# Edge stage of a graph layer: one loaded number a step for ScalarE's copies, and TensorE's per-step numbers worked out in registers

## The reference, cut to what matters

```python
e = el[src] + er[dst]
e = jnp.where(e >= 0, e, NEG_SLOPE * e)
e_max = jax.ops.segment_max(e, dst, num_segments=N)
exp_e = jnp.exp(e - e_max[dst])
denom = jax.ops.segment_sum(exp_e, dst, num_segments=N)
a = exp_e / jnp.maximum(denom[dst], 1e-16)
msg = feat_v[src] * a[:, :, None]
rst = jax.ops.segment_sum(msg, dst, num_segments=N)
```

## Time and profile before

| | before |
|---|---|
| median of 3 runs | 3522.52 us (3513.96 to 3525.18) |
| the profiled execution | 3480.26 us, span 3478.4 us |
| PE (matmuls) busy | 2417.5 us (69%) |
| DVE busy | 1829.6 us (53%) |
| POOL busy | 1338.1 us (38%) |
| ACT busy | 909.8 us (26%) |
| granted TensorE clock, mean | 0.809 |

### The profile page before, as it was taken

One profiled execution on the slowest core, in us unless ns is written; L12 is line 12 of the kernel. 1 busy time (PEld: TensorE's weight loads), 2 busy tenths in 40 slices (PEclk: granted clock), 3 DMA queues, 4 the chain that ended last, 5 costly groups with the idle time before them and its releaser, 6 DMA issues. The chain is left out here.

```text
span 3478.4 us, 50828 instructions
## 1 busy us (share of the span) xinstructions
PE 2417.5 (69%) x11245; PEld 1803.3 (52%) x11246; DVE 1829.6 (53%) x3903; ACT 909.8 (26%) x1917; POOL 1338.1 (38%) x1406
## 2 busy tenths in 40 slices
PE   3899998666777877777877777777233329999500
PEld 3677776223555555555555555555233328888400
DVE  5544443786666655566556655565353334444433
ACT  0111111011333333333333333333443313333100
POOL 0000000302565555565556555652144342222244
PEclk8899998898888878888788878889555559999755
DMA  3122222644555555655656556653655634444576
GB/s 115 49 68 68 68 68 77 228 167 134 165 162 159 157 164 163 169 160 154 169 164 171 166 154 173 170 163 89 221 134 136 131 76 134 145 145 145 168 257 232
DMA packets 238264, 507.89 MB, mean 146 GB/s; under 512 B 50320, under 2 KB 76432, under 8 KB 238208
## 3 DMA queue, kind: packets, MB, share of 16 engines
q0 software_dynamic: 85936, 274.85, 28.6%
q1 hardware_dynamic: 134752, 196.94, 18.5%
q10 hardware_dynamic: 17520, 35.44, 3.0%
HBM read 394.73 MB, written 112.37 MB: 146 GB/s over the span
## 5 line engine op out<-in xcount | busy, mean ns | idle before, releaser
L618 POOL DMA_INDIRECT arena<-v_table,idx x832 | 917.2, 1102 | 847.1 <-PE ps L1566 670.1
L1566 PE MATMUL ps<-arena 128*128 128x260 f32 x3328 | 975.4, 441 | 315.9 <-issue 289.6
L1566 PEld LDWEIGHTS ps<-arena 128*128 128x128 f32 x3328 | 678.5, 216 | 533.2 <-issue 427.7
L757 ACT ACTIVATE arena<-ps x832 | 501.9, 603 | 1096.2 <-PE ps L1566 668.4
L1182 DVE TENSOR_TENSOR arena<-arena 128x512 f32<-128x512 f32 x832 | 547.1, 683 | 0.0
L1384 PE MATMUL ps<-arena 128*128 (+4 forms) x1994 | 423.8, 336 | 94.3 <-DMA arena<-q_table 73.8
L1389 PE MATMUL ps<-ident,arena 128*128 128x128 f32 x1128 | 213.8, 308 | 328.1 <-DVE arena L1257 257.2
L1384 PEld LDWEIGHTS ps<-arena 128*128 128x128 f32 (+1 forms) x1994 | 275.7, 195 | 224.8 <-issue 115.3
L1389 PEld LDWEIGHTS ps<-ident,arena 128*128 128x128 f32 x1128 | 151.0, 159 | 349.3 <-DVE arena L1257 262.2
L658 POOL DMA_INDIRECT arena<-xn_table,e_idx x105 | 99.3, 945 | 281.5 <-PE ps L1389 265.0
L595 POOL TENSOR_SCALAR ag<-ag 128x1 f32<-128x1 f32 x49 | 10.7, 219 | 502.3 <-DVE ag L999 502.2
(11 more groups left out here) (282 smaller groups left out, 3470.0 us busy)
## 6 DMA issues: line engine op xcount, KB each, us to landing
y_table<-arena SPq DMA_DIRECT2D x105, 256.0 KB, 2.5
arena<-local_table ACTq DMA_DIRECT2D x52, 512.0 KB, 4.2
arena<-in_x SPq DMA_DIRECT2D x98, 256.0 KB, 2.7
arena<-v_table,idx POOLq DMA_INDIRECT x832
v_table<-arena SPq DMA_DIRECT2D x49, 260.0 KB, 2.9
agg<-arena SPq DMA_DIRECT2D x49, 260.0 KB
arena<-agg SPq DMA_DIRECT2D x49, 260.0 KB, 4.6
x_mix<-arena SPq DMA_DIRECT2D x49, 256.0 KB, 2.7
```

The costliest lines, as they stand in the source:

```text
L618: pool.indirect_dma_start(vg[:, j % 2 * U + i, :], None, v_table, bass.IndirectOffsetOnAxis(ap=idx[:, j, i:i + 1], axis=0))\
L757: act.activation(halves(fin[:, bass.ds(dst_, DH)], HALF), halves(ps[:, bass.ds(src_, 2 * D)], D)[:, :, 0:HALF], ACT.Copy).then_inc(s("act_ ...
L1566: last = pe.matmul(ps[:, bass.ds(acc + h * D, HALF)], hot[:, i // V % 2, i % V, :], vg[:, b * U + i, h * HALF:(h + 1) * HALF], start=False ...
```

## The change

Tables: the tables pe_tab, act_tab, d_tab and chunk_tab go. In their place stand first_tab (the tile of each chunk's first step), turn_tab (16 bits for each chunk, one for each step that ends a tile), and room_tab (for ScalarE, one number a step, from which it takes both where to read and where to write). `fin` now has its slots at the same distances as the accumulators and two of them in place of four.

ScalarE: one load of 16 numbers for a chunk; a copy waits for its own copy before and for the matmuls of the step after, and no longer for tile_sum and for the stores. TensorE: for each two chunks it loads four tiles and four bit rows; it works out each step's accumulator, turn and next tile in registers, and in `expanded` the tile of each of the 16 matmuls; at the end of a tile it waits in addition for the stores. The preparation of the next chunk is put after later steps: on TensorE from after 1, 3, 5, 8, 10 to after 5, 7, 9, 12, 11 (`turned_max` now behind `factors`), on VectorE from after 2, 4, 6, 9, 12 to after 5, 7, 9, 11, 13. VectorE builds the first one-hot matrix of a chunk ahead of its wait for the weights (`found`).

```diff
-            def snapshots(t, n):
-                places = looked_up(ENGINE.Activation, act_tab, t * 2, 2 * n, DUMMY * D)
-                counts = looked_up(ENGINE.Activation, act_tab, t * 2 + 2 * ST, 2 * n, 32768)
...
+            def snapshot(t, room):
+                if later(t, 1):
+                    act.wait_ge(*past("act_step", t))
+                act.wait_ge(s("step_mm"), t + 2)
+                act.activation(halves(fin[:, bass.ds(room, DH)], HALF), halves(ps[:, bass.ds(room, 2 * D)], D)[:, :, 0:HALF],
+                               ACT.Copy).then_inc(s("act_step"), 1)
...
+                rooms = looked_up(ENGINE.Activation, room_tab, c * U, U, DUMMY * D)
+                for i in range(U):
+                    snapshot(c * U + i, rooms[i])
+                    if not more:
+                        continue
+                    if i == 8:
+                        factor(c + 1)
+                    elif i == 11:
+                        weights(c + 1, 1 - b)
...
-                    if i == 2:
+                    if i == 5:
                         scored(c + 1, n, q)
-                    elif i == 4:
+                    elif i == 7:
                         run_max(c + 1, n)
-                    elif i == 6:
+                    elif i == 9:
                         linked(c + 1)
-                    elif i == 9:
+                    elif i == 11:
                         joined_max(c + 1, n)
-                    elif i == 12:
+                    elif i == 13:
                         shifted(c + 1, n)
...
-                for i, d in enumerate(tiles):
+                for i in range(U):
                     last = product(prep[:, i * 3 * H:(i + 1) * 3 * H],
-                                   [(hot_t[:, i * P:(i + 1) * P], er_flat[:, bass.ds(d * 3 * H, 3 * H)])])
+                                   [(hot_t[:, i * P:(i + 1) * P], er_flat[:, bass.ds(d * (3 * H), 3 * H)])])
+                    if i < U - 1:
+                        d = next_tile(pe, d, turn_of(pe, bits, i))
...
-            def step(t, i, b):
-                if i % V == 0:
-                    marks[:] = looked_up(ENGINE.PE, pe_tab, t * 2, 2 * V + 1, 2 * D)
-                acc, turn, other = marks[i % V * 2:i % V * 2 + 3]
+            def step(t, i, b, d, turn):
+                acc = held(pe, (d & 1) * (2 * D), 2 * D)
+                other = held(pe, (acc + 2 * D) & (4 * D - 1), 2 * D)
                 pe.wait_ge(s("step_pv"), t + 1)
...
                 with pe.If(turn):
-                    empty(acc, False, True).then_inc(s("tile_sum"), 1)
-                    freed, = looked_up(ENGINE.PE, pe_tab, t + (2 * ST + 2), 1, ST)
+                    empty(acc, False, True)
+                    pe.wait_ge(s("fin_st"), d * 16 + past("fin_st", -16)[1])
+                    freed, = looked_up(ENGINE.PE, tile_tab, d, 1, past("act_step", ST)[1])
                     pe.wait_ge(s("act_step"), freed)
...
-                    if i == U - 1 and ahead:
-                        tiles = tiles_of(c + 2)
-                    step(c * U + i, i, b)
+                    turn = held(pe, (bits >> i) & 1, 1)
+                    after = held(pe, d + turn, NT - 1)
+                    step(c * U + i, i, b, d, turn)
+                    d = after
```

More of the change, by code:

```diff
@@ L60 @@
[L60 to L64, removed]
@@ L745, in weights, with chunk @@
                 act.activation(score_cols(b), score_cols(b), ACT.Exp).then_inc(s("p_exp"), 1)
-            def snapshots(t, n):
-                places = looked_up(ENGINE.Activation, act_tab, t * 2, 2 * n, DUMMY * D)
-                counts = looked_up(ENGINE.Activation, act_tab, t * 2 + 2 * ST, 2 * n, 32768)
[L750 to L760, removed]
+            def snapshot(t, room):
[4 more added lines that the diff above has]
+                               ACT.Copy).then_inc(s("act_step"), 1)
+            def chunk(c, b, r, own):
                 more = not (isinstance(c, int) and c == NCH - 1)
@@ L779, in _ @@
             weights(0, 0)
-            chunks(act, chunk)
+            chunks(act, chunk, lambda c, n: (None,) * n, 0)
             act.wait_ge(s("step_mm"), ST)
@@ new lines, in _ @@
+            step_of(last)
+            in_chunks = [row_.rearrange("o (c i) -> o c i", i=U) for row_ in (turn, aux)]
+            step_of(dve.tensor_tensor(in_chunks[1], in_chunks[0], power_row.unsqueeze(1).broadcast_to([1, NCH, U]), ALU.mult))
+            step_of(dve.tensor_reduce(bits, in_chunks[1], AX.X, ALU.add))
+            dve.tensor_copy(turn_tab[0:1, 0:NCH], bits)
+            dve.memset(turn_tab[0:1, NCH:NCH + 2], 0)
+            dve.tensor_copy(first_tab[0:1, 0:NCH], d_r[:, 0:ST:U])
@@ L1226, in _ @@
             turned_hot(1, 1, 0)
[L1227 removed]
+            chunks(dve, chunk, lambda c, n: chunk_places(ENGINE.DVE, c, n), 0)
             def weights_lo(c):
@@ L1609, in _ @@
             turned_max(0)
-            expanded(1, tiles_of(1))
-            empty(0, True, False).then_inc(s("tile_sum"), 1)
-            chunks(pe, chunk, lambda c, n: looked_up(ENGINE.PE, chunk_tab, c, n, 2 * D))
-            empty((NT - 1) % 2 * 2 * D, False, True).then_inc(s("tile_sum"), 1)
+            expanded(1, *begun[1])
+            empty(0, True, False)
+            chunks(pe, chunk, lambda c, n: chunk_places(ENGINE.PE, c, n), 2)
+            pe.wait_ge(*past("fin_st", 16 * (NT - 2)))
+            empty((NT - 1) % 2 * 2 * D, False, True).then_inc(s("step_mm"), 1)
             def logits(t):
```

167 lines of the change are left out of this document (78 added, 89 removed).

## The result

The changed kernel takes 3714.65 us (median of 4 runs, 3701.60 to 3720.55) against 3518.80 for the kernel before (4 runs, 3513.96 to 3525.18): a ratio of 1.055, with a 95% interval of 1.052 to 1.059. It is slower by 5.5%, outside the forecast of 3450 to 3690; the direction was right. Two repeats gave 1.053 (1.050 to 1.056) and 1.055 (1.052 to 1.058).

A forecast was written before the change was run, and what follows sets the result against it. The prediction took TensorE's sequencer to bound the kernel. Its terms summed to +1.6 us a chunk (+82 us), with -9 for the prologue: 3553 us profiled, scaled to a forecast of 3595 us, range 3450 to 3690.

The forecast's parts named there:

- What bounds the kernel: Edge stage: TensorE sets the pace, and within TensorE its sequencer; a chunk takes 30.9 us.
- The price of 0.10 us: TensorE's sequencer: one register instruction costs 0.10 us, within 0.04 to 0.12.
- Steps 0 to 4: TensorE, chunk's start: a load goes and the slow clock hides some register work, -1.6 us a chunk.
- Steps 4 to 8: TensorE: register work about equals the load it replaces, plus two small matmuls, +0.2 us a chunk.
- Steps 8 to 12: TensorE: register work worth the load, plus a stall at step 12 behind VectorE's wait for ScalarE's exponential, +2.0 us a chunk.
- B: Rival: the clock falls a second time within the chunk; 3655 us for half the chunks, 3710 for nearly all; chance 0.15.
- A: Main case, the whole kernel: the summed terms hold, slower by 1 to 3.5%, 3595 us; chance 0.50.
- Steps 12 to 15: TensorE: the load of 16 numbers and its idle array go, -2.1 us a chunk.
- Step 15 to the next step 0: TensorE, chunk's boundary: 29 register instructions in `expanded` and two loads at the loop's turn, +2.8 us a chunk.
- The prologue: Before the projection: fewer VectorE table rows ahead of TensorE's first matmul, -9 us in all.
- F: Rival: TensorE's longer loop fetches instructions at each turn, 48 us more, 3643 us; chance 0.03.
- ScalarE at nothing: ScalarE's shorter loads gain nothing, since it mostly waits for TensorE, which sets the pace.

The follow-up runs named there:

- e7: The kernel before with eight idle register instructions more ahead of each TensorE step: 4008.60 us, 1.151 of the kernel before.
- e9: The kernel before with four idle register instructions more ahead of each TensorE step: 3750.52 us, 1.077 of the kernel before.
- v2: New version, old link places: TensorE loads only accumulators, takes tile ends from bits; ScalarE's load split in four: 3472.09 us, 0.983 of the kernel before.
- e2: The kernel before with only the later places of the chunk's links, all loads kept: 3645.36 us, 1.037 of the kernel before.
- e10: The kernel before with eight idle register instructions more ahead of each ScalarE copy, TensorE unchanged: 3560.41 us, 1.022 of the kernel before.
- e1: The changed kernel with the links back in their old places, TensorE's numbers still from registers: 3700.59 us, 1.053 of the kernel before.
- e4: The changed kernel with TensorE's numbers loaded and links in old places, leaving ScalarE's part and the prologue: 3506.70 us, 0.997 of the kernel before.
- e3: The changed kernel with TensorE's numbers loaded again, links in the later places: 3642.91 us, 1.037 of the kernel before.
- a1: The changed kernel, unchanged, run again on another chip: 3721.93 us, 1.053 of the kernel before.
- a0: The kernel before, unchanged, profiled on the same chip as a1: 3534 us in its one run.
- e6: The changed kernel with the steps' numbers loaded, registers only for the 16 small matmuls of `expanded`: 3670.90 us, 1.039 of the kernel before.
- e8: The kernel before with TensorE's loop over four chunks an iteration in place of two: 3557.01 us, 1.021 of the kernel before.
- b1: The changed kernel with links in old places and ScalarE's load of 16 numbers split into four: 3712.72 us, 1.051 of the kernel before.
- c2: The program of e9 again, on a chip of the slower kind: 3778.24 us, 1.069 of the kernel before.

## Why the prediction was wrong, step by step

- **What bounds the kernel: right, but not alone.** e7 and e9 make TensorE's sequencer slower, and the chunk follows in proportion; v2 makes it faster, and the kernel is. But e2 and e10 leave what TensorE does in a step as it is and cost 3.7 and 2.2%: the chain of hand-overs has next to no slack either.
- **The price of 0.10 us: right.** It had given 250 us more for e9 and 500 for e7, counted on a kernel before of 3515 us; beside the 3483 of their group they took 267 and 525 us more.
- **Steps 0 to 4, -1.6: -3.5.** Mis-sized in parts. The registers alone give -2.0 here (5.93 in e1, 7.96 in e4). The rest is `gathered_ends`, which used to stand behind step 3 and went to step 7 with its wait; the places alone also give -2.0 (6.00 in e3).
- **Steps 4 to 8, +0.2: +1.4.** In e1, with the link elsewhere, it is +0.1 (5.35 against 5.20), so the register part was right. What was left out is that the wait that leaves step 3 arrives at step 7.
- **Steps 8 to 12: the step that failed, +2.0: +4.5.** The prediction took the register work there as worth the load, put "a stall at step 12" of 2.0 us, and priced nothing else. e1, without the later places, loses 3.4 us here against e4: the register work costs far more than the load here, by stalls and not by its price alone. The wait for the exponential is there (102.7 us, 42 times, 2.4 each), and the time from step 11 to 12 grows by 0.9 us, not 2.0. More is lost at steps 8, 9 and 10, which take 2.66, 2.44 and 1.76 us where they took 1.12, 0.88 and 1.30. Two things are seen there. One is the register rows of 0.7 us, nearly half of them ahead of step 8, with an idle array (up to 3.75 us): in a1 the array stands still for over 0.3 us ahead of steps 8 to 11, with the step's rows weighed before, 61 times; 45 of these stalls (118.0 us) overlap a sequencer row over 0.5 us, 16 (16.0 us) don't. The other is the slow clock behind them, in which 38, 70, 69 and 56% of the matmul records of steps 8 to 11 start in a1 and none in a0. The forecast held B, a second fall of the clock in the chunk, at 0.15, with a price of +61 us for half the chunks and 3710 for nearly all. It happened, and earlier in the chunk than B had it; that B's 3710 is near the measured 3715 is partly luck, since the idle array of steps 8 to 11 is no part of its price. It should have come with A, not beside it: A itself put a new wait of 2 us into the chunk.
- **Steps 12 to 15, -2.1: -1.6**, with 7 to 19% of those matmuls still at the slow clock.
- **Step 15 to the next step 0, +2.8: +3.2.** Right in kind; e6 shows the exchange of +3.4 against -3.3 at step 14. The 16 matmuls spread over 5.5 us as forecast; before it was 1.3, not 2.
- **The prologue, -9: right.** The projection's first matmul starts at 89.80 us, 99.85 before.
- **F, fetches at the loop's turn: did not happen**, but the branch back of e8's longer body waits 5.3 us a turn, which fits it.
- **ScalarE at nothing: too bold.** e10 shows that it has no room of 0.8 us a step. e4 shows that the edit itself costs nothing while TensorE loads its numbers. With registers, which make steps 0 to 4 faster, ScalarE's load of 16 numbers comes late: splitting it takes step 8 to 9 from 3.06 us (e1) to 1.68 (b1).
- **Total.** The five stretches miss by -1.9, +1.2, +2.5, +0.5 and +0.4 us; less the 0.3 for ends of tiles, which is inside them here, that is 2.4 us a chunk or 125 us, and 3595 + 125 = 3720. The forecast took the one profile of before, 3480 us, up to the median by a factor (1.012; the 1.021 printed there is the ratio of 3595 to 3522.52). That profile lies 1.2% below the median of the runs beside it, and on a chip of its speed no register row is over 0.1 us. Nothing in it could show the rows of 0.7 us.

What is shown: each half of the change loses alone; the price of an instruction; that the stall moves when one cause of it is relieved. What was only seen together: a stretch of register instructions without a pause, and the rows of 0.7 us. In a1 TensorE's sequencer rows over 0.3 us are 139 us in all, of which the array covers a part. How much of the loss would be left without them, and what makes them, stays open; the last section has what the traces say of it.

## What to carry to other kernels

Compare a load to registers with the instructions that replace it one number at a time: 0.236 us a number against 0.10 us an instruction makes two instructions for a number nearly a loss, and one a gain. A load ahead of a group can also hide behind the matmuls that are queued, while instructions at every step use up the sequencer's lead: in the median step its row stands 0.70 us ahead of the matmul in the kernel before, 0.32 in the changed one and 0.12 in e1. And when a forecast adds a wait of microseconds to TensorE's path, the slow clock behind it belongs to the same sum.

## What the runs showed of the hardware that was not expected

- Single register instructions of 0.7 us (up to 1.4), on the sequencers of TensorE, ScalarE and SyncE, never VectorE or GpSimd, in every profile taken where the kernel before takes 3514 us or more, and in none of those where it takes 3483 (and not in the first profile of before, 3480). When TensorE has them, ScalarE often has them at the same microsecond (1598.52 and 1600.65 beside 1597.11 to 1599.94), and right behind them TensorE's sequencer goes through rows of 13 to 22 ns. That looks like something that the engines share.
- The same profiles also lack records. The trace of before has 41,435 updates of semaphores, that of a0, the same program, 31,908; e9 has 41,460 and c2, the same program, 33,797. All five profiles without a row of 0.7 us on any engine have 41,430 to 41,463, all fifteen others 29,739 to 33,797. So a wait that these traces put down to "issue" can be one whose update is missing.
- The time that such a row bears is not always when the instruction ran: the matmul of step 8 starts at 1600.71, the sequencer's row ahead of it at 1601.37. In the first profile of the changed kernel 33 step matmuls start before that row, by up to 1.37 us; in before and in e7 to e10 none does, and each is at least 0.097 us behind it.
- Of the fifteen profiles with missing records, the eight with 62 to 229 register rows over 0.2 us on TensorE have 17.3 to 17.6 recorded instructions a us on all engines over the edge stage, the other seven 14.7 to 17.0. Where the kernel before takes 3483 us or less, 17.3 (before) and 20.6 (e10) go without such a row.
- These three speak for the recording, which would be held up where rows stand close together. A wait for instructions to be fetched, which the expectations call starving, would not by itself put a matmul ahead of its own row or lose updates. Every run here comes with a span and a granted clock, so each was recorded, the timed ones too. The Trainium skill, in "NOTIFIC — the notification-queue block", section "7.1 Overflow: three behaviours, one of which stalls the engine", says that the inner pipeline of the block that writes the records pushes back rather than lose a record inside the block, and that its count of stalls would tell that an engine had been held up. That would fit the late rows, but it does not tell where the missing updates went. No run here could leave the recording away, so it is not shown, and how much of the 5.5% would stay without it is not known.
- A loop body of TensorE twice as long as that of before (e8) makes the branch back 5.3 us long instead of 0.21; 433 sequencer rows a turn in place of 200 (the changed kernel) do not.
- The same program differs by 1 to 1.5% between chips, in a way that a single profile doesn't tell.
